# Value products of an attention kernel kept whole, in other banks, with the orders of a pair of units rewritten

## The chip, the cores and the metric

The kernel runs on one core of a Trainium2 chip. The core has five engines with an instruction stream of their own each: TensorE (PE, matrix products into PSUM), VectorE (DVE), ScalarE (ACT), GpSimd (POOL) and SyncE (SP, which issues DMAs). They wait for each other through semaphores alone, and within an engine instructions run in the order in which they are written. The metric is the time of one execution on the device in microseconds (us); lower is better.

## What is computed

```python
def _L0_xattn_ref(query, kv, Wq, bq, Wkv, bkv, Wo, bo):      # query: layernorm(x), 32 x 64 x 512; kv: ctx
    q = (query @ Wq + bq).reshape(B, L, NKV, G, HDIM)         # 8 key heads, 4 query heads each, HDIM 128
    k_, v_ = jnp.split(kv @ Wkv + bkv, 2, axis=-1)
    ...
    scores = jnp.einsum('blkgd,bmkd->bkglm', q, k) * scale
    attn = jax.nn.softmax(scores, axis=-1)
    o = jnp.einsum('bkglm,bmkd->blkgd', attn, v).reshape(B, L, NHEAD * HDIM)
    return o @ Wo + bo
...
x = x + _L0_xattn_ref(_layernorm(x), ctx, ...)
x = x + _L0_ffn_ref(_layernorm(x), router_w, router_b, A, Bm)   # 8 low-rank experts, best 2 of each token
```

## The kernel before

All is in float32. Each product that needs full accuracy is made of passes of rounded parts: a factor is split into a high part (made on ACT, `high`, L819) and a low part (the rest: source minus high part, made on DVE, L1155, or on POOL, L592), and PE multiplies high by high, low by high and high by low (L1675 to L1677).

The work goes over 8 groups (one key head and its 4 query heads) of 4 units of 512 tokens (8 batch rows of 64). Two units are a **duo**, d; its units are 2d and 2d+1. A group has two duos, p=0 and p=1; the loop runs groups 1 to 6, both duos of group 7 stand written out behind it, and `opening()` does the first two duos. Each engine has its own function `duo(g, p)`, in which the order is written by hand; nothing is scheduled by a planner. In duo d four things overlap:

- **Query products** of duo d: seven products of a Strassen-like scheme (`product(k, r)`, k = 1, 6, 2, 7, 4, 5, 3, in two halves r) instead of eight. ACT copies the first (`first_product`), DVE adds the others up (`y_sum`, `z_sum`, `w_sum`, `query_sum`) to the four blocks c11, c21 (unit 2d) and c12, c22 (unit 2d+1); ACT makes their high part (`query_high`), POOL the low part (`query_low`).
- **Scores** of units 2d and 2d+1, each in two halves c (`scores(d, k, c)`), into the four banks `att`.
- **Softmax** of each half (u, c): ACT copies half of the scores (`copy_half`), DVE adds the other half (`s_add`), transposes and takes the row maximum (`s_max`), ACT swaps partitions (`swap_max`, four short copies), DVE takes the peak (`s_peak`), POOL subtracts (`shift`), ACT exponentiates (`exponents`), DVE sums (`s_sum`), ACT swaps (`swap_sum`), DVE inverts (`s_inverse`, two short instructions), POOL multiplies (`normalise`), DVE transposes back (`p_turn`), ACT and POOL split the result (`probs_high`, `probs_low`). Halves c of successive units use the same memory, so `copy_half(u+1, c)` comes behind `p_turn(u, c)`.
- **Value products** of units 2d-2 and 2d-1 (`outputs(u, c)`, twelve matmuls of 256 columns) into the two banks `turn`, split on ACT (`output_high`) and DVE (`output_low`), and the eight **output tiles** of these units (`out(d, p, j)`, j = 0 to 3 and 4 to 7), which DVE adds to `y` (`add`).

PSUM's other banks are a `ring` of four, which query products and output tiles share. In the second duo of a group ACT and POOL also split Wo, and, but in the last group, DVE combines the next group's query weights (`combine_w`, L1208 to L1216, in `parts` from `raw`) and ACT and POOL split these (`split_q`). The last group's second duo also begins the statistics of the second layernorm. SP's queue loads blocks of x (`load_block`), keys, values and weights in a fixed order, each behind a semaphore.

On PE, value products stood alone between query products or output tiles: c=0 of unit 2d-2 behind product (6,1), c=1 behind (4,0), c=0 of unit 2d-1 behind `scores(d, 0, 1)`, c=1 behind `out(d, p, 3)`.

## Time and profile before

| | |
|---|---|
| time, median of 3 runs | 1061.63 us (1060.66 to 1062.37) |
| profiled execution, its own time | 1060.89 us |
| span of its records | 1058.7 us |
| PE, DVE, POOL, ACT busy | 98%, 76%, 64%, 53% of the span |
| granted TensorE clock, mean | 0.995 of full |

Busy shares are means over the whole span. Ends of matmuls are modelled and overlap, so the spacing of PE's work is read from starts. A row of a timeline may merge several equal instructions (x2, x4); `<-` before a name says which engine and line ended an idle time.

### The profile page before, as it was taken

The numbers are of one execution on the slowest core, as the hardware profiler recorded it, in microseconds if no ns is written. First come the engines' busy times: TensorE is split into PE (matmuls) and PEld (weight loads), VectorE is DVE, ScalarE is ACT, GpSimd is POOL, SyncE is SP. The second block draws the span as 40 slices with busy tenths as digits, with TensorE's granted clock in tenths as the row PEclk, the third lists the DMA queues.
The fourth block names the chain that finished last, engine by engine and source line by source line (L and its number), as shares of the span: only waits on it lengthen the run. The fifth ranks groups of instructions, "written<-read, shape, count | busy, mean of one in ns | idle before, by whom it ended". The sixth has DMA issues, their size and how long they took to land.

```text
span 1058.7 us, 17316 instructions
## 1 busy us (share of the span) xinstructions
PE 1035.8 (98%) x5409; PEld 850.4 (80%) x5409; DVE 802.0 (76%) x1420; ACT 557.2 (53%) x1314; POOL 674.5 (64%) x563
## 2 busy tenths in 40 slices
PE   8999999988999999999999999999999999999996
PEld 7878887867788888888888888888888888887884
DVE  3563455469987887797788878877987797788986
ACT  3122113257756665665567566666665575665420
POOL 1286237768876787677578767866786787574300
PEclk9999999999999999999999999999999999999998
DMA  8647963995364655546282827364554637240013
GB/s 310 208 129 256 317 212 82 394 352 200 130 255 149 220 179 187 204 152 258 99 290 89 314 96 261 133 234 143 213 218 148 241 115 270 94 154 11 2 41 120
DMA packets 85657, 197.99 MB, mean 187 GB/s; under 512 B 10560, under 2 KB 43368, under 8 KB 70384
## 3 DMA queue, kind: packets, MB, share of 16 engines
q1 hardware_dynamic: 83072, 181.73, 49.4%
q10 hardware_dynamic: 2544, 15.73, 3.7%
q8 instruction: 23, 0.38, 0.1%
q14 instruction: 18, 0.15, 0.0%
HBM read 161.78 MB, written 35.65 MB: 186 GB/s over the span
## 4 chain that ended last, share of the span: by engine, by line
PE 79%; DVE 9%; DMA 6%; POOL 3%; issue 1%; ACT 1%; SPq 1%; ACTq 0%; DVEq 0%
PE banks L1675 23%; PE banks L1676 22%; PE banks L1677 22%; PE banks L1815 5%; PE banks L1798 2%; PE banks L1799 2%; DMA k_raw<-keys_dram 2%; PE banks L1700 1%; DMA values_dram<-parts 1%; DMA keys_dram<-parts 1%; DVE stats L1230 1%; DMA raw<-in_L_xattn_Wq_dram 1%; DVE xo L1155 1%; POOL w_l L592 1%; DMA raw<-in_L_xattn_Wkv_dram 1%
## 5 line engine op out<-in xcount | busy, mean ns | idle before, releaser
L1675 PE MATMUL banks<-wo_h,xo 128*128 128x512 f32 x512 | 204.5, 399 | 0.0
L1676 PE MATMUL banks<-wo_l,xo 128*128 128x512 f32 x512 | 200.5, 392 | 0.0
L1677 PE MATMUL banks<-wo_h,xo 128*128 128x512 f32 x512 | 199.9, 390 | 0.0
L592 POOL TENSOR_TENSOR qT_l<-parts,qT_h 128x512 fp32r<-128x512 f32 x128 | 165.4, 1298 | 52.1 <-ACT qT_h L819 52.1
L1675 PE MATMUL banks<-xo,w_h 128*128 128x512 f32 x448 | 179.0, 400 | 2.5 <-DVE parts L1280 1.9
L1676 PE MATMUL banks<-xo,w_h 128*128 128x512 f32 x448 | 175.7, 392 | 0.0
L1677 PE MATMUL banks<-xo,w_l 128*128 128x512 f32 x448 | 174.4, 389 | 0.0
L592 POOL TENSOR_TENSOR xo<-sT,xo 128x512 fp32r<-128x512 f32 (+1 forms) x72 | 102.6, 1425 | 75.5 <-ACT xo L819 75.5
L1155 DVE TENSOR_TENSOR xo<-banks,xo 128x512 fp32r<-128x512 f32 (+1 forms) x156 | 100.8, 665 | 31.2 <-ACT xo L819 30.7
L1675 PEld LDWEIGHTS banks<-wo_h,xo 128*128 128x128 f32 x512 | 96.5, 188 | 23.5 <-issue 0.2
L1303 DVE SCALAR_TENSOR_TENSOR parts<-banks,g_bias,parts 128x512 f32<-128x512 f32 x128 | 94.6, 741 | 26.8 <-PE banks L1677 24.4
L1677 PEld LDWEIGHTS banks<-wo_h,xo 128*128 128x128 f32 x512 | 96.4, 188 | 21.0
L1676 PEld LDWEIGHTS banks<-wo_l,xo 128*128 128x128 f32 x512 | 96.6, 189 | 18.3
L819 ACT ACTIVATE xo<-banks 128x512 fp32r<-128x512 f32 (+1 forms) x156 | 84.8, 581 | 39.8 <-PE banks L1815 21.8
L819 ACT ACTIVATE qT_h<-parts 128x512 fp32r<-128x512 f32 x128 | 80.2, 629 | 47.8 <-DVE parts L1303 46.1
L1350 DVE TENSOR_TENSOR y<-banks,y 128x512 f32<-128x512 f32 x120 | 81.2, 682 | 31.4 <-PE banks L1677 30.8
L625 POOL TENSOR_TENSOR low_or_x<-low_or_x,row_sum 128x512 f32<-128x512 f32 x64 | 70.5, 1102 | 53.7 <-DVE row_sum L1339 53.7
L1675 PEld LDWEIGHTS banks<-xo,w_h 128*128 128x128 f32 x448 | 84.2, 188 | 24.0 <-DVE parts L1280 2.3
L618 POOL TENSOR_TENSOR low_or_x<-low_or_x,row_max 128x512 f32<-128x512 f32 x64 | 70.2, 1097 | 47.1 <-DVE row_max L1325 46.0
L1677 PEld LDWEIGHTS banks<-xo,w_l 128*128 128x128 f32 x448 | 84.1, 188 | 18.6
L1676 PEld LDWEIGHTS banks<-xo,w_h 128*128 128x128 f32 x448 | 84.2, 188 | 15.2
L917 ACT COPY low_or_x<-banks 64x512 f32<-64x512 f32 x64 | 37.3, 583 | 109.3 <-PE banks L1799 109.2
(145 smaller groups left out, 2269.4 us busy)
## 6 DMA issues: line engine op xcount, KB each, us to landing
xo<-x_dram SPq DMA_DIRECT2D x105, 1024.0 KB, 5.0
x_dram<-xo ACTq DMA_DIRECT2D x14, 1024.0 KB, 11.9
values_dram<-parts SPq DMA_DIRECT2D x64, 128.0 KB, 2.9
keys_dram<-parts SPq DMA_DIRECT2D x32, 256.0 KB, 5.0
k_raw<-keys_dram SPq DMA_DIRECT2D x32, 256.0 KB, 4.9
raw<-in_L_xattn_Wo_dram SPq DMA_DIRECT2D x8, 1024.0 KB, 8.0
v_raw<-values_dram SPq DMA_DIRECT2D x64, 128.0 KB, 3.7
raw<-in_L_xattn_Wkv_dram SPq DMA_DIRECT2D x7, 1024.0 KB, 6.7
```

Source lines behind the costliest of these rows:

```text
L592: return nc.gpsimd.tensor_tensor(dst, src, high_part.bitcast(F32), ALU.subtract)
L618: nc.gpsimd.tensor_tensor(s[:, blocks, :], s[:, blocks, :], row_max[:, blocks].unsqueeze(2).broadcast_to([P, D // QR, QR]), ALU.subtract). ...
L625: nc.gpsimd.tensor_tensor(s[:, blocks, :], s[:, blocks, :], row_sum[:, blocks].unsqueeze(2).broadcast_to([P, D // QR, QR]), ALU.mult).then ...
L819: return nc.scalar.activation(dst, src, ACT.Copy)
L917: act.copy(half[L:P, c], att_s[L:P, :, 0, :])
L1155: return nc.vector.tensor_tensor(dst, src, high_part.bitcast(F32), ALU.subtract)
L1303: nc.vector.scalar_tensor_tensor(out=slot_of(c, r), in0=product_of(d, p, k, r), scalar=q_bias(c, r), in1=slot_of(what, r), op0=ALU.add, op ...
L1350: nc.vector.tensor_tensor(y[:, t, :], ring[:, slot, :], y[:, t, :], ALU.add).then_inc(y_added, 1)
L1675: mm(dst, stat[0], mov[0], start=start, stop=False)
L1676: mm(dst, stat[0], mov[1], start=False, stop=False)
L1677: return mm(dst, stat[1], mov[0], start=False, stop=stop)
L1815: last = mm(turn[:, i, n % 2 * G * L:(n % 2 + 1) * G * L], v[keys_of, n, :], p[keys_of, n, :], start=p is pT_h and v is v_h, stop=p is pT_l)
```

## The change

Value products are made whole: both halves c of a unit follow each other on PE. Unit 2d-2 has its place behind product (7,1); unit 2d-1 behind `out(d, p, 3)`, and behind it follow product (3,1) and `scores(d, 0, 1)`, which stood earlier. One half of each unit goes to other banks (`value_bank`): c=0 of unit 2d-2 into the score banks, c=1 of unit 2d-1 into ring slots 2 and 3. Ring slots become fixed per duo (`OUT_SLOTS`), with other semaphores waited for. The orders on ACT, DVE and POOL are rewritten to this, `query_high` of c12 r=1 comes last (`HIGHS`), weight combinations and their splits move, and combination 2 lies in another part of memory (slot 2 of `parts` instead of 0). In the tail's order DVE has the first output lows ahead of a row maximum. The opening and the work of each instruction are as before.

```diff
+OUT_SLOTS = (2, 3, 1, 0, 0, 1, 2, 3)
+PV_SLOTS = (2, 3)
...
+            return isinstance(d, int) and d < DUOS
+
+        def product_slot(d, p, k, r):
+
+            return ((DUO_TASKS * p if opening_duo(d) else 0) + PROD_AT[k, r]) % RING
+
+        def out_slot(d, p, j):
+
+            return (DUO_TASKS * p + len(PROD) + j) % RING if opening_duo(d) else OUT_SLOTS[j]
+
+        def value_bank(d, k, c, i):
+
+            if d is not None and k == 0 and c == 0:
+                return att[:, i, :]
+            if d is not None and k == 1 and c == 1:
+                return ring[:, PV_SLOTS[i], :]
+            return turn[:, i, :]
...
+                if split:
+                    split_q(g + 1, [0, 2], False)
+                normalise(2 * d, 0)
                 query_low(d, "c12", 1)
                 keys_low(2 * d + 1)
+                if split:
+                    split_q(g + 1, [1], False)
                 shift(2 * d, 1)
-                normalise(2 * d, 0)
...
-                    split_q(g + 1, [0], False)
+                    split_q(g + 1, [3], False)
                 values_low(2 * d)
...
-                output_high(2 * d - 2, 0, 0)
-                output_high(2 * d - 2, 0, 1)
                 query_high(d, "c11", 0)
                 swap_sum(2 * d - 1, 0)
                 wo_high_part(3)
                 query_high(d, "c11", 1)
                 exponents(2 * d - 1, 1)
                 swap_sum(2 * d - 1, 1)
-                output_high(2 * d - 2, 1, 0)
+                output_high(2 * d - 2, 0, 0, d, 0)
+                output_high(2 * d - 2, 0, 1, d, 0)
+                output_high(2 * d - 2, 1, 0, d, 0)
+                output_high(2 * d - 2, 1, 1, d, 0)
                 query_high(d, "c21", 0)
-                output_high(2 * d - 2, 1, 1)
...
+                query_high(d, "c12", 0)
+                query_high(d, "c22", 1)
+                probs_high(2 * d - 1, 1)
                 copy_half(2 * d, 0)
                 if split:
                     split_q(g + 1, [0], False)
-                probs_high(2 * d - 1, 1)
-                query_high(d, "c12", 0)
-                query_high(d, "c12", 1)
-                copy_half(2 * d, 1)
                 swap_max(2 * d, 0)
-                query_high(d, "c22", 1)
-                output_high(2 * d - 1, 0, 0)
-                output_high(2 * d - 1, 0, 1)
-                swap_max(2 * d, 1)
                 exponents(2 * d, 0)
-                keys_high(2 * d + 1)
-                output_high(2 * d - 1, 1, 0)
-                output_high(2 * d - 1, 1, 1)
-                swap_sum(2 * d, 0)
-                exponents(2 * d, 1)
                 if split:
                     split_q(g + 1, [2], False)
+                swap_sum(2 * d, 0)
+                output_high(2 * d - 1, 0, 0, d, 1)
+                output_high(2 * d - 1, 0, 1, d, 1)
+                output_high(2 * d - 1, 1, 0, d, 1)
+                output_high(2 * d - 1, 1, 1, d, 1)
+                copy_half(2 * d, 1)
+                query_high(d, "c12", 1)
+                keys_high(2 * d + 1)
+                if split:
+                    split_q(g + 1, [1, 3, 5], False)
+                swap_max(2 * d, 1)
+                probs_high(2 * d, 0)
+                exponents(2 * d, 1)
+                copy_half(2 * d + 1, 0)
+                swap_sum(2 * d, 1)
                 values_high(2 * d)
-                swap_sum(2 * d, 1)
-                probs_high(2 * d, 0)
-                copy_half(2 * d + 1, 0)
                 if split:
-                    split_q(g + 1, [1, 3, 5, 4, 6], False)
+                    split_q(g + 1, [4, 6], False)
                 probs_high(2 * d, 1)
                 if not last:
+                    swap_max(2 * d + 1, 0)
                     copy_half(2 * d + 1, 1)
-                if not last:
-                    swap_max(2 * d + 1, 0)
...
-                        dve.wait_ge(q_low, 16 * g)
+                        dve.wait_ge(q_low, 16 * g - 8 + LOW_AT["c21", 0])
                     ins = nc.vector.tensor_tensor(s1, w_block(1, 0), w_block(1, 1), ALU.add)
...
                     ins = nc.vector.tensor_tensor(s3, w_block(0, 0), w_block(1, 0), ALU.subtract)
                 else:
                     dve.wait_ge(combined, 4 * g + 2)
...
@@ -1262,7 +1285,7 @@
...
                 s_peak(2 * d - 1, 1)
                 query_sum(d, p, "c11", 0)
                 query_sum(d, p, "c11", 1)
-                output_low(2 * d - 2, 0, 0)
-                output_low(2 * d - 2, 0, 1)
                 s_inverse(2 * d - 1, 0)
                 z_sum(g, d, p, 0)
                 z_sum(g, d, p, 1)
                 s_sum(2 * d - 1, 1)
                 query_sum(d, p, "c21", 0)
+                output_low(2 * d - 2, 0, 0, d, 0)
+                output_low(2 * d - 2, 0, 1, d, 0)
                 query_sum(d, p, "c21", 1)
                 p_turn(2 * d - 1, 0)
                 w_sum(d, p, 0)
                 query_sum(d, p, "c22", 0)
                 w_sum(d, p, 1)
-                output_low(2 * d - 2, 1, 0)
+                output_low(2 * d - 2, 1, 0, d, 0)
                 query_sum(d, p, "c22", 1)
                 s_inverse(2 * d - 1, 1)
-                add(0)
-                output_low(2 * d - 2, 1, 1)
+                output_low(2 * d - 2, 1, 1, d, 0)
                 p_turn(2 * d - 1, 1)
                 query_sum(d, p, "c12", 0)
+                if split:
+                    combine_w(g + 1, 1, False)
+                add(0)
                 s_add(2 * d, 0)
-                query_sum(d, p, "c12", 1)
                 s_max(2 * d, 0)
                 add(1)
-                s_add(2 * d, 1)
                 s_peak(2 * d, 0)
-                s_max(2 * d, 1)
-                output_low(2 * d - 1, 0, 0)
-                output_low(2 * d - 1, 0, 1)
+                if split:
+                    combine_w(g + 1, 2, False)
                 add(2)
-                s_peak(2 * d, 1)
                 s_sum(2 * d, 0)
                 if split:
-                    combine_w(g + 1, 1, False)
-                output_low(2 * d - 1, 1, 0)
+                    combine_w(g + 1, 3, False)
                 add(3)
-                if split:
-                    combine_w(g + 1, 2, False)
+                output_low(2 * d - 1, 0, 0, d, 1)
+                output_low(2 * d - 1, 0, 1, d, 1)
                 s_inverse(2 * d, 0)
-                output_low(2 * d - 1, 1, 1)
-                s_sum(2 * d, 1)
+                output_low(2 * d - 1, 1, 0, d, 1)
+                query_sum(d, p, "c12", 1)
+                output_low(2 * d - 1, 1, 1, d, 1)
+                s_add(2 * d, 1)
+                s_max(2 * d, 1)
                 p_turn(2 * d, 0)
-                if split:
-                    combine_w(g + 1, 3, False)
                 add(4)
-                add(5)
-                if last:
-                    ln_stats("f", 0)
-                s_inverse(2 * d, 1)
+                s_peak(2 * d, 1)
                 if split:
                     combine_w(g + 1, 4, False)
+                if last:
+                    add(5)
+                    for t in range(3):
+                        tile_stats("f", t)
+                s_sum(2 * d, 1)
                 s_add(2 * d + 1, 0)
+                s_inverse(2 * d, 1)
+                if last:
+                    tile_stats("f", 3)
+                    ln_combine("f", 0)
+                if not last:
+                    add(5)
+                    s_max(2 * d + 1, 0)
+                if not last:
+                    add(6)
                 p_turn(2 * d, 1)
                 if not last:
-                    add(6)
-                    s_max(2 * d + 1, 0)
                     add(7)
-                if not last:
                     s_add(2 * d + 1, 1)
 
 
...
+                elif (k, r) == (3, 1) and not opening_duo(d):
+                    pe.wait_ge(y_added, d * 8 - 8 + 3)
...
+                if k == 0 and c == 0 and not opening_duo(d):
+                    pe.wait_ge(o_low, (2 * d - 2) * 4 + 2)
...
-            def outputs(u, c):
+            def outputs(u, c, d=None, k=None):
 
                 pe.wait_ge(v_low, u + 1)
                 pe.wait_ge(p_low, u * 2 + c + 1)
-                if not isinstance(u, int) or u > 0 or c > 0:
+                if d is not None and k == 0 and c == 0:
+                    pe.wait_ge(s_added, u * 2 + 4)
+                elif d is not None and k == 1 and c == 1:
+                    pe.wait_ge(y_added, d * 8 - 8 + 2)
...
-                            last = mm(turn[:, i, n % 2 * G * L:(n % 2 + 1) * G * L], v[keys_of, n, :], p[keys_of, n, :],
+                            last = mm(value_bank(d, k, c, i)[:, n % 2 * G * L:(n % 2 + 1) * G * L], v[keys_of, n, :], p[keys_of, n, :],
                                       start=p is pT_h and v is v_h, stop=p is pT_l)
                             if n % 2 and p is pT_l:
                                 last.then_inc(o_filled, 1)
 
             def out(d, p, j):
 
-                if j < 4:
+                if opening_duo(d) and j < 4:
                     pe.wait_ge(summed, d * len(SUMS) + SUM_AT[("c22", "c12")[j // 2], j % 2])
+                elif opening_duo(d):
+                    pe.wait_ge(y_added, d * 8 - 8 + j - 4 + 1)
+                elif j in (0, 1, 2, 3, 5):
+                    name, r = {0: ("c22", 0), 1: ("c22", 1), 2: ("c21", 1), 3: ("c12", 0), 5: ("c12", 1)}[j]
+                    pe.wait_ge(summed, d * len(SUMS) + SUM_AT[name, r])
+                elif j == 4:
+                    pe.wait_ge(y_added, d * 8 - 8 + 4)
                 else:
-                    pe.wait_ge(y_added, d * 8 - 8 + j - 4 + 1)
-                out_project(2 * d - 2 + j // UT, out_slot(p, j), j % UT)
+                    pe.wait_ge(o_low, (2 * d - 1) * 4 + 3 + j - 6)
+                out_project(2 * d - 2 + j // UT, out_slot(d, p, j), j % UT)
 
             def opening():
...
                 product(g, p, 6, 0)
                 product(g, p, 6, 1)
-                outputs(2 * d - 2, 0)
                 product(g, p, 2, 0)
                 product(g, p, 2, 1)
                 product(g, p, 7, 0)
                 product(g, p, 7, 1)
+                outputs(2 * d - 2, 0, d, 0)
+                outputs(2 * d - 2, 1, d, 0)
                 product(g, p, 4, 0)
-                outputs(2 * d - 2, 1)
                 product(g, p, 4, 1)
                 product(g, p, 5, 0)
                 product(g, p, 5, 1)
@@ -1899,13 +1945,13 @@
                     pe.wait_ge(wo_low, (STEPS + g) * KC + KC)
                 out(d, p, 0)
                 scores(d, 0, 0)
-                product(g, p, 3, 1)
                 out(d, p, 1)
-                scores(d, 0, 1)
-                outputs(2 * d - 1, 0)
                 out(d, p, 2)
                 out(d, p, 3)
-                outputs(2 * d - 1, 1)
+                outputs(2 * d - 1, 0, d, 1)
+                outputs(2 * d - 1, 1, d, 1)
+                product(g, p, 3, 1)
+                scores(d, 0, 1)
                 out(d, p, 4)
                 out(d, p, 5)
                 scores(d, 1, 0)
```

Three places show how instructions move. First PE in the first duo of a group, around the value products of unit 2d-2. Before (L1677 is a query product, L1815 the value product; ISA and REGISTER_ALU are the sequencer's):

```order
L1677 MATMUL banks<-xo,w_l 128x512
L1805 ISA
L1806 ISA
L1808 REGISTER_ALU
L1815 MATMUL banks<-xo,v_h 128x256 x2
L1815 MATMUL banks<-xo,v_l 128x256 x2
L1815 MATMUL banks<-xo,v_h 128x256 x4
L1815 MATMUL banks<-xo,v_l 128x256 x2
L1815 MATMUL banks<-xo,v_h 128x256 x2
L1761 REGISTER_ALU
L1764 REGISTER_ALU
```

In the changed kernel (its line numbers are larger by some tens: L1706 query product, L1854 value product):

```order
L1854 MATMUL banks<-xo,v_h 128x256 x2
L1854 MATMUL banks<-xo,v_l 128x256 x2
L1854 MATMUL banks<-xo,v_h 128x256 x4
L1854 MATMUL banks<-xo,v_l 128x256 x2
L1854 MATMUL banks<-xo,v_h 128x256 x2
L1839 REGISTER_ALU
L1845 REGISTER_ALU
L1854 MATMUL banks<-xo,v_h 128x256 x2
L1854 MATMUL banks<-xo,v_l 128x256 x2
L1854 MATMUL banks<-xo,v_h 128x256 x4
L1854 MATMUL banks<-xo,v_l 128x256 x2
L1854 MATMUL banks<-xo,v_h 128x256 x2
```

A second value product follows at once; before, another query product came first.

Then ACT in the same duo, around `copy_half(2d, 0)` (COPY low_or_x, two rows). `qT_h<-parts` are high parts of c blocks, `xo<-sT` those of probabilities. Before, from c22 r=0 on:

```order
L819 ACTIVATE qT_h<-parts 128x8x64
L819 ACTIVATE xo<-sT 128x512
L916 ISA
L917 COPY low_or_x<-banks 64x512
L918 COPY low_or_x<-banks 64x512
L819 ACTIVATE xo<-sT 128x512
L881 REGISTER_ALU
L819 ACTIVATE qT_h<-parts 128x8x64
L881 REGISTER_ALU
L819 ACTIVATE qT_h<-parts 128x8x64
```

In the changed kernel:

```order
L837 ACTIVATE qT_h<-parts 128x8x64
L837 ACTIVATE xo<-sT 128x512
L899 REGISTER_ALU
L837 ACTIVATE qT_h<-parts 128x8x64
L899 REGISTER_ALU
L837 ACTIVATE qT_h<-parts 128x8x64
L837 ACTIVATE xo<-sT 128x512
L934 ISA
L935 COPY low_or_x<-banks 64x512
L936 COPY low_or_x<-banks 64x512
```

The copy moved behind both halves' probabilities of unit 2d-1 and behind two more high parts.

Last DVE in the second duo of a group, behind the peak of (2d, 0) (row_max<-row_max,other). `parts<-...raw` are weight combinations, row_sum the row sum, y an output tile's add. Before, further down, combination 1 stands behind a row sum:

```order
L1325 TENSOR_TENSOR row_max<-row_max,other 128x16
L1331 TENSOR_REDUCE row_sum<-low_or_x 128x16
L1202 ISA
L1207 REGISTER_ALU
L1208 TENSOR_TENSOR parts<-raw 128x512
L1354 REGISTER_ALU
L1155 TENSOR_TENSOR xo<-banks,xo 128x2x4x64
L1350 TENSOR_TENSOR y<-banks,y 128x512
L1210 ISA
```

In the changed kernel combination 2 stands behind the peak:

```order
L1348 TENSOR_TENSOR row_max<-row_max,other 128x16
L1229 ISA
L1231 REGISTER_ALU
L1232 TENSOR_TENSOR parts<-parts,raw 128x512
L1373 TENSOR_TENSOR y<-banks,y 128x512
L1354 TENSOR_REDUCE row_sum<-low_or_x 128x16
L1234 TENSOR_TENSOR parts<-raw 128x512
L1373 TENSOR_TENSOR y<-banks,y 128x512
```

Combination 2 moved up to the peak, and combination 3 to the place behind the row sum.

## Rows read from the trace of the kernel before

**Rows 1.** The page's shares: busy us, share of the span, instructions of each engine
```profile
PE 1035.8 (98%) x5409; PEld 850.4 (80%) x5409; DVE 802.0 (76%) x1420; ACT 557.2 (53%) x1314; POOL 674.5 (64%) x563
```

**Rows 2.** Windows of two successive duos: busy us of PE, PEld, DVE, ACT, POOL; clock, DMA
```profile
477.57:526.90 49.33, 49.33 (x263) 40.51 (x261) 39.31 (x69) 28.22 (x70) 34.26 (x29) 1.00 0.52 191
526.90:576.22 49.32, 49.32 (x262) 40.50 (x261) 41.92 (x69) 33.79 (x81) 38.17 (x31) 1.00 0.53 191
```

**Rows 3.** Timeline of PE around a value product: start, us, engine, line, operation
```profile
531.91 0.39 PE L1676 MATMUL banks<-xo,w_h 128*128 128x512 f32 x1
...
532.14 0.39 PE L1677 MATMUL banks<-xo,w_l 128*128 128x512 f32 x1
...
532.46 0.38 PE L1815 MATMUL banks<-xo,v_h 64*128 64x256 f32 x2
...
532.68 0.28 PE L1815 MATMUL banks<-xo,v_l 64*128 64x256 f32 x2
...
533.36 0.50 PE L1675 MATMUL banks<-xo,w_h 128*128 128x512 f32 x1
...
533.70 0.40 PE L1676 MATMUL banks<-xo,w_h 128*128 128x512 f32 x1
```

**Rows 4.** Instructions by line and shape over both duos: busy, mean ns, idle before
```profile
L1303 DVE SCALAR_TENSOR_TENSOR parts<-banks,g_bias,parts 128x512 f32<-128x512 f32 x16 | 11.9, 742 | 3.9 <-PE banks L1677 3.8
...
L819 ACT ACTIVATE qT_h<-parts 128x512 fp32r<-128x512 f32 x16 | 10.1, 630 | 5.6 <-DVE parts L1303 5.3
...
L1320 DVE TENSOR_REDUCE row_max<-low_or_x 128x16 f32<-128x512 f32 x9 | 6.2, 686 | 0.3
...
L1344 DVE STREAM_TRANSPOSE sT<-low_or_x 128x512 f32<-128x512 f32 x8 | 5.7, 707 | 0.1
...
L1313 DVE TENSOR_TENSOR sT<-banks,low_or_x 64x512 f32<-64x512 f32 x8 | 5.6, 695 | 0.1
...
L1155 DVE TENSOR_TENSOR xo<-banks,xo 128x512 fp32r<-128x512 f32 x16 | 10.5, 677 | 1.2 <-ACT xo L819 1.1
...
L927 ACT ACTIVATE low_or_x<-low_or_x 128x512 f32<-128x512 f32 x8 | 5.0, 630 | 0.8 <-POOL low_or_x L618 0.5
...
L917 ACT COPY low_or_x<-banks 64x512 f32<-64x512 f32 x8 | 4.7, 583 | 15.3 <-PE banks L1799 15.3
...
L910 ACT COPY other<-row_max 32x16 f32<-32x16 f32 x16 | 3.2, 202 | 3.4 <-DVE row_max L1320 3.2
...
L1339 DVE RECIPROCAL row_sum<-row_sum 128x16 f32<-128x16 f32 x8 | 2.0, 253 | 0.3
...
L1465 DVE COPY g_bias<-bias 128x4 f32 x1 | 0.2, 170 | 0.0
```

**Rows 5.** Timeline of DVE in two places
```profile
484.43 0.68 DVE L1331 TENSOR_REDUCE row_sum<-low_or_x 128x16 f32<-128x512 f32 x1
...
485.02 0.83 DVE L1325 TENSOR_TENSOR row_max<-row_max,other 128x16 f32<-128x16 f32 x1
...
562.77 1.28 DVE L1208 TENSOR_TENSOR parts<-raw 128x512 f32<-128x512 f32 x1
```

**Rows 6.** Timeline of ACT: two activations in a row
```profile
502.56 0.63 ACT L819 ACTIVATE xo<-sT 128x512 fp32r<-128x512 f32 x1
503.11 0.63 ACT L819 ACTIVATE qT_h<-parts 128x512 fp32r<-128x512 f32 x1
```

**Rows 7.** Timeline of POOL in the places of rows 5
```profile
483.26 2.56 POOL L592 TENSOR_TENSOR w_l<-parts,w_h 128x512 fp32r<-128x512 f32 x2
...
559.91 1.05 POOL L618 TENSOR_TENSOR low_or_x<-low_or_x,row_max 128x512 f32<-128x512 f32 x1
...
563.46 1.50 POOL L618 TENSOR_TENSOR low_or_x<-low_or_x,row_max 128x512 f32<-128x512 f32 x1
```

**Rows 8.** DMA issues: tensor, queue, count, KB each, median us to landing
```profile
xo<-x_dram SPq DMA_DIRECT2D x105, 1024.0 KB, 5.0
...
raw<-in_L_xattn_Wq_dram SPq DMA_DIRECT2D x7, 1024.0 KB, 5.6
```

More of the change, by code:

```diff
@@ L63 @@
 SUM_AT = {name: n + 1 for n, name in enumerate(SUMS)}
-HIGHS = [("c11", 0), ("c11", 1), ("c21", 0), ("c21", 1), ("c22", 0), ("c12", 0), ("c12", 1), ("c22", 1)]
+HIGHS = [("c11", 0), ("c11", 1), ("c21", 0), ("c21", 1), ("c22", 0), ("c12", 0), ("c22", 1), ("c12", 1)]
 HIGH_AT = {name: n + 1 for n, name in enumerate(HIGHS)}
@@ L765, in duo @@
                 if split:
[L766 removed]
+                    split_q(g + 1, [6], False)
             split_wo(0, range(KC))
@@ L876, in first_product @@
                     act.wait_ge(q_low, d * 8 - 4)
-                act.copy(slot_of("x", r), ring[:, product_slot(p, 1, r), :]).then_inc(copied, 1)
+                act.copy(slot_of("x", r), ring[:, product_slot(d, p, 1, r), :]).then_inc(copied, 1)
             def query_high(d, c, r):
@@ L1210, in combine_w @@
                     dve.wait_ge(combined, 4 * g + 1)
+                    if not first:
+                        dve.wait_ge(q_low, 16 * g - 8 + LOW_AT["c12", 0])
                     ins = nc.vector.tensor_tensor(s2, s1, w_block(0, 0), ALU.subtract)
@@ L1215, in combine_w @@
                     dve.wait_ge(combined, 4 * g + 2)
+                    if not first:
+                        dve.wait_ge(q_low, 16 * g - 8 + LOW_AT["c22", 1])
                     ins = nc.vector.tensor_tensor(s4, w_block(0, 1), s2, ALU.subtract)
```

49 lines of the change are left out of this document (24 added, 25 removed), and 2 rows, old and new, of the table VECTOR_TAIL.

## The prediction

> **What bounds the kernel now.** I read the page's shares first: TensorE (PE) is busy for 98% of the span [rows 1]. Then the windows of two successive duos in the middle of the main loop: PE is busy for 49.33 of 49.33 us and for 49.32 of 49.32, the granted clock is full, while VectorE (DVE) has 39.3 and 41.9, GpSimd (POOL) 34.3 and 38.2, ScalarE (ACT) 28.2 and 33.8 [rows 2]. So in the loop nothing is waited for on PE, and its 14 duos are 14 x 49.33 = 690.6 us of the 1058.7 us span. An edit there can win in two ways only: less PE time, or nothing. It can lose wherever another engine now comes later than PE.
>
> **What PE saves.** The reader is to look at starts, since ends of matmuls are modelled. A 512-column matmul follows the last by 0.23 us; the one ahead of a value product is followed after 0.32; the twelve value matmuls take 0.90, of which the first two 0.22; and the first matmul behind them is followed after 0.34 [rows 3]. Leaving and entering thus costs 0.09 + 0.11, some 0.06 more in the next ten matmuls, and inside the block 0.1 at the first and 0.1 at the last pair, since the four steady pairs between take about 0.115 each: 0.46 per block. Two of four blocks in a duo now follow directly on another, and the switch from scores to a value product goes: 2 x 0.46 = 0.9 less, 48.45 us a duo. If PE stays the bound that is 14 x 0.88 = 12.3 us.
>
> **What the other engines then need.** The new order ties the three elementwise engines into one chain that goes round once per duo and touches PE nowhere decisively. I follow it from the start of the DVE sum for c12, half r=0 (time 0). Durations are those of [rows 4]; followers on one engine start closer than they last: DVE 0.60 apart [rows 5], ACT 0.54 [rows 6]. A handover between engines I take as 0.03 (the stall of a peak that I come to ends 0.03 after its cause [rows 5, 7]), to POOL 0.08.
>
> First stretch, the half (2d,0). The sum lasts 0.74. ACT then has three activations in a row before `copy_half(2d,0)`, which stood ahead of all three: 0.74 + 0.03 + 3 x 0.54 = 2.39. Copy 0.60 + 0.58 (to 3.57), s_add 0.70 + 0.73 (5.02), transpose and row maximum 0.74 + 0.69 (6.45), swap of four copies 0.85 (7.33), peak, which ends at 7.65 (below), shift 1.05 (8.78), exponent 0.63 (9.44), row sum 0.68 (10.15), swap 0.87: the first `output_high` of unit 2d-1 starts at 11.06. Before, two of the four stood ahead of that exponent and two ahead of that swap; now all four stand behind both. Its DVE half starts at 11.69, the second at 12.29 and ends at 12.97. `out(d,4)` waits for it. On PE that tile is 12.4 us behind the first scores (three output tiles, two value blocks, one query product, one score half); so at once it is late by several tenths, even if everything else were early.
>
> Second stretch. DVE: low, low, inverse (0.21 + 0.17), low, c12 r=1, low take 3.45; s_add of half (2d,1) starts at 15.14. Add and row maximum 2.87, p_turn and one add 1.3, peak 19.32, shift, exponent at 20.66, and only behind that exponent ACT copies the scores of (2d+1,0): s_add 22.4. Then inverse 0.46, an add, row maximum, an add, p_turn at 26.84 (1.42 + 0.46 + 0.6 + 1.34 + 0.6), probs_high 0.63, swap 0.87, and only then `copy_half(2d+1,1)`: its s_add starts at 30.31. PE passed the end of the duo at about 26.0 (out4 at 13.15 + 12.84 us of the rest), so this half is some 4 us behind its scores.
>
> Third stretch, in the next duo. s_add 1.42, peak, y 0.7, row maximum 1.34, y 0.6, row sum 0.6: peak at 34.97, held by POOL to 35.6; c11 0.74, its activation 0.66, swap 0.88, inverse at 37.86; two z sums and the row sum 2.4, swap 0.87: `output_high` at 41.16, low at 41.79. Then nine DVE instructions to the inverse, 5.8, normalise 1.05, p_turn, and the next c12 sum at 49.8.
>
> So one turn takes 49.8 us where PE needs 48.45 and needed 49.33. PE's own events lie clear of it: c21 r=0 needs product (4,0), which arrives at 40.35, and has until 41.1.
>
> **The port between DVE and POOL.** A DVE peak of 16 elements lasted 0.83 us, from 485.02 to 485.85, and POOL's running pair of low parts ended at 485.82 [rows 5, 7]. In the other direction, a DVE combination of two SBUF operands ran from 562.77 to 564.05, and the POOL shift begun at 563.46 took 1.50 instead of 1.05 [rows 5, 7]. So peaks and inverses (two SBUF inputs) wait for POOL's running instruction, and weight combinations hold back POOL. Both bear on the chain now. Peak (2d,0) finds the last of four low parts running; the peak of (2d-1,1) finds a Wo or key part. In the six duos that also split the next group's weights, combinations 2 and 4 stand directly behind a peak whose shift the chain waits for: 0.35 and 0.32 each, and combination 3 (up to 0.4) ahead of the add and low behind it. The duo after such a one has the group's bias copy (0.17 [rows 4] and its own wait, 0.3 together) and an inverse that meets a low part (0.45). 49.8 becomes 51.1 there, 0.5 of it with even chances either way.
> The Trainium skill (SBUF — State Buffer, "Who interferes with whom") says that a DVE instruction with two SBUF inputs and a GpSimd instruction that reads SBUF exclude each other for the whole instruction, whichever began first. The trace agrees in kind. By that rule each shift would be held for all of a combination (0.68), which adds 0.35 x 2 x 6 = 4 us to the sum; I keep the 0.45 that the row shows as the most.
>
> **The sum.** From the loop's first product to the first c12 sum 23.1 us (there PE still leads: product (4,0) at 14.3, then 8.7 of DVE); 7 turns of 49.8 and 6 of 51.1, 655.2; from the last c12 sum to PE's end of the loop 26.0: 704.3. That is 13.6 more than 690.6. The tail's first low part and p_turn come about 0.5 later in relation to PE. The profiled execution took 1060.9 us (0.7 under the median of 1061.6), so 1075.0 for its like, and I say 1075.
>
> **Edits costed at nothing.** Value products in score and ring banks wait for s_add of (2d-1,1), for add 1 and for older low parts; by the walk these end 5, 1.5 and 10 us before PE asks; product (3,1) needs add 2 and has only some tenths, which fall into PE's wait ahead of the fifth tile in any case. POOL's new places for split parts lie where it waits for an inverse. The blocks for products 2 and 7 of the next duo are issued behind product (3,1), which moves from 25 to 34.6 us in its duo; they land within 5.0 us [rows 8] and are needed at 53.9. Combination 1 now stands at 0.7, and the next group's raw weights are issued 6.9 before time 0 and land in 5.6 [rows 8]: at worst it starts some tenths later and still ends before s_add at 3.6. The SP queue holds no other issue behind these that anyone needs sooner. If this cover fails, the whole wait adds, since combination, add and s_add are in one queue.
>
> **Rivals.** (1) The chain is shorter than I walked and PE stays the bound: faster. For: DVE is busy for only 41.9 of 49.3 us in the fuller duo [rows 2], and 70 steps with 0.02 us of error each one way would make 1.4 us. Against: the durations repeat to a few ns. At best 1061.6 - 12.3 = 1049.3; but even with the first and third stretch free, low parts held back to 12.97 bind PE through product (4,0), c21 and the c12 sum in 48.9 a duo, which gives 1055.6. (2) The chain turns in about 49.3: 1061 to 1063, no change to be told. (3) The port's coin flips all fall badly: the inverse at 37.86 just misses POOL's gap and waits for the next low part (1.25 us, 7 times), combination 3 waits for a split part (0.8, 6 times): 13.6 us more at most, half of it likely in that case: 1083. It decides where two instructions are ready within 0.05 us of each other. (4) The change removes no switch, as PE cannot run two value blocks back to back because the second waits for its bank: then even (1) is void and the time is that of the chain, 1075.
>
> **How the numbers follow.** My forecast 0.55 (1066 to 1081 by itself); (3) 0.19; (2) 0.10; (1) 0.16. (4) changes none of these, since the chain sets the time. What can be told from no change is about 0.2%, 2.1 us. Faster 0.16, same 0.10, slower 0.74. The range leaves out about 0.13 below and 0.07 above: 1056 to 1088.
>
> **What the profile will show.** Right: in the loop PE waits once or twice per duo, above all ahead of the fifth output tile for the DVE low part and slightly ahead of the first; ACT hardly waits for scores any more (its copies waited 15.3 us for them in two duos [rows 4]); a duo takes 49.8 to 51.5. Joined value blocks take about 1.6 us for 24 matmuls. Wrong: a loop of 48.5 to 49.2 us per duo with PE fully busy; or PE waiting for a DMA, or at half clock, which I expect nowhere new in the loop.

## The result and the profile after

The changed kernel takes 1094.15 us (median of 4 runs, 1091.17 to 1094.61) against 1061.14 for the kernel before in the same session: 1.0319 times as long, 95% interval 1.0301 to 1.0337. The forecast was 1075.0 with a range to 1088: right in its sign and in what it said would wait, too small by 19 us and outside its range.

The page's shares, to be held against [rows 1]:

```profile
PE 1038.0 (95%) x5409; PEld 853.2 (78%) x5409; DVE 798.1 (73%) x1420; ACT 557.2 (51%) x1314; POOL 671.1 (62%) x563
```

No engine has more instructions, and only PE and its weight loads are busy for longer (by 2.2 and 2.8 us); all have a smaller share of a span of 1088.9 us. Windows cut at the start of the c12 r=0 sum, the point from which the prediction walked its chain ("a turn"): first the turn from a group's first duo into its second, then the one that starts in the second and splits weights (columns as in [rows 2]):

```profile
716.08:767.19 51.11, 49.38 (x262) 40.43 (x261) 38.70 (x67) 30.26 (x74) 33.53 (x29) 1.00 0.47 170
767.19:819.42 52.23, 50.14 (x262) 41.57 (x261) 41.60 (x73) 31.73 (x77) 38.34 (x32) 0.97 0.56 195
```

The turns alternate between 51.1 and 52.2, where before a duo took 49.33 and the walk had said 49.8 and 51.1. PE now waits; its two dearest waits over the whole run (us in total, how often, the longest):

```profile
PE banks L1704 <- DVE xo L1174: 20.5, 16, 2.1
...
PE banks L1704 <- DVE parts L1326: 8.6, 10, 0.9
```

The first is mostly the fifth output tile waiting for its low part, the second the first output tile. The copies of scores on ACT, which waited 15.3 us in two duos [rows 4], wait no more (last columns: idle time ahead and its cause):

```profile
L935 ACT COPY low_or_x<-banks 64x512 f32<-64x512 f32 x8 | 4.6, 581 | 0.2
```

The place that decides. The first inverse of a group's second duo on DVE, and POOL at the same time:

```profile
754.13 1.28 DVE L1359 TENSOR_TENSOR row_sum<-row_sum,other 128x16 f32<-128x16 f32 x1 [0.90 <-ACT other L929]
```

```profile
753.08 1.06 POOL L632 TENSOR_TENSOR low_or_x<-low_or_x,row_max 128x512 f32<-128x512 f32 x1
754.09 1.30 POOL L606 TENSOR_TENSOR qT_l<-parts,qT_h 128x512 fp32r<-128x512 f32 x1
```

POOL began the c11 low part at 754.09; the inverse was released at 754.13, 0.04 later, and lasted until POOL was done (755.39): 1.28 us for 16 elements a row. It is so in all seven turns that end in a second duo: 0.04 or 0.05 behind POOL, 1.28 or 1.29 long.

In the split turn, combinations 2 (L1232) and 3 (L1234) on DVE, and POOL beside them:

```profile
774.69 0.18 DVE L1348 TENSOR_TENSOR row_max<-row_max,other 128x16 f32<-128x16 f32 x1 [0.19 <-ACT other L929]
774.89 0.69 DVE L1232 TENSOR_TENSOR parts<-parts,raw 128x512 f32<-128x512 f32 x1
...
777.79 1.80 DVE L1234 TENSOR_TENSOR parts<-raw 128x512 f32<-128x512 f32 x1
```

```profile
774.95 1.54 POOL L632 TENSOR_TENSOR low_or_x<-low_or_x,row_max 128x512 f32<-128x512 f32 x1 [0.21 <-DVE row_max L1348]
776.45 1.30 POOL L606 TENSOR_TENSOR w_l<-raw,w_h 128x512 fp32r<-128x512 f32 x1
777.75 1.29 POOL L606 TENSOR_TENSOR w_l<-parts,w_h 128x512 fp32r<-128x512 f32 x1
...
787.94 1.43 POOL L632 TENSOR_TENSOR low_or_x<-low_or_x,row_max 128x512 f32<-128x512 f32 x1 [0.44 <-DVE row_max L1348]
```

Combination 2 holds the shift back by 0.49 (1.54 for 1.05), and combination 3 again comes 0.04 after POOL has begun: 1.80 instead of 0.69. Combination 4, behind the next peak, holds the shift of (2d,1) by 0.38 (the last line, 1.43 for 1.05).

On PE, the joined value product (to be held against [rows 3]):

```profile
753.41 0.38 PE L1854 MATMUL banks<-xo,v_h 64*128 64x256 f32 x2
...
755.02 0.50 PE L1704 MATMUL banks<-xo,w_h 128*128 128x512 f32 x1
```

From 753.41 to 755.02 it is 1.61 us for 24 matmuls; twice 0.90 before.

### The profile page after: what moved, and what is told of

The parts are those of the page before. It is cut to its first block, busy times and chain, and to the rows that moved or that the text cites. A ratio compares the mean times of both kernels' runs of the same rounds, so it can differ in the third digit from the quotient of the medians.

```text
span 1088.9 us, 17332 instructions
## 1 busy us (share of the span) xinstructions
PE 1038.0 (95%) x5409; PEld 853.2 (78%) x5409; DVE 798.1 (73%) x1420; ACT 557.2 (51%) x1314; POOL 671.1 (62%) x563
## 4 chain that ended last, share of the span: by engine, by line
DVE 39%; PE 16%; issue 14%; POOL 12%; ACT 10%; DMA 6%; DVEq 1%; SPq 1%; ACTq 0%; POOLq 0%
PE banks L1704 5%; DVE parts L1326 5%; PE banks L1706 5%; PE banks L1705 5%; DVE xo L1174 4%; POOL low_or_x L632 3%; DVE sT L1336 3%; DVE low_or_x L1341 3%; DVE y L1373 3%; DVE sT L1367 2%; DVE sT L1335 2%; POOL qT_l L606 2%; DVE row_sum L1359 2%; DVE row_sum L1354 2%; ACT xo L837 2%
## 5 line engine op out<-in xcount | busy, mean ns | idle before, releaser
L1706 PE MATMUL banks<-wo_h,xo 128*128 128x512 f32 x512 | 201.5, 394 | 0.0
L1706 PE MATMUL banks<-xo,w_l 128*128 128x512 f32 x448 | 174.4, 389 | 0.0
L1704 PEld LDWEIGHTS banks<-wo_h,xo 128*128 128x128 f32 x512 | 97.7, 191 | 56.0 <-DVE xo L1174 20.1
L1706 PEld LDWEIGHTS banks<-wo_h,xo 128*128 128x128 f32 x512 | 97.5, 190 | 21.3
L639 POOL TENSOR_TENSOR low_or_x<-low_or_x,row_sum 128x512 f32<-128x512 f32 x64 | 67.7, 1058 | 71.0 <-DVE row_sum L1362 71.0
L632 POOL TENSOR_TENSOR low_or_x<-low_or_x,row_max 128x512 f32<-128x512 f32 x64 | 72.7, 1136 | 54.8 <-DVE row_max L1348 53.6
L1706 PEld LDWEIGHTS banks<-xo,w_l 128*128 128x128 f32 x448 | 84.1, 188 | 18.2
L1705 PEld LDWEIGHTS banks<-xo,w_h 128*128 128x128 f32 x448 | 84.2, 188 | 15.3
L1335 DVE TENSOR_TENSOR sT<-banks,low_or_x 64x512 f32<-64x512 f32 x64 | 43.7, 683 | 70.5 <-ACT low_or_x L936 69.8
L837 ACT ACTIVATE xo<-sT 128x512 fp32r<-128x512 f32 (+1 forms) x72 | 48.5, 674 | 90.0 <-DVE sT L1367 56.0
L837 ACT ACTIVATE xo<-banks 128x512 fp32r<-128x512 f32 (+1 forms) x156 | 80.8, 590 | 21.3 <-PE banks L1729 8.6
```

The source lines that it names most:

```text
L632: nc.gpsimd.tensor_tensor(s[:, blocks, :], s[:, blocks, :], row_max[:, blocks].unsqueeze(2).broadcast_to([P, D // QR, QR]), ALU.subtract). ...
L639: nc.gpsimd.tensor_tensor(s[:, blocks, :], s[:, blocks, :], row_sum[:, blocks].unsqueeze(2).broadcast_to([P, D // QR, QR]), ALU.mult).then ...
L837: return nc.scalar.activation(dst, src, ACT.Copy)
L1335: nc.vector.tensor_tensor(whole[0:L], att_s[0:L, :, 0, :], half[L:P, c], ALU.add)
L1704: mm(dst, stat[0], mov[0], start=start, stop=False)
L1705: mm(dst, stat[0], mov[1], start=False, stop=False)
```

## The experiments

Each kernel ran five times (E5 and E8 twelve times); there is no E7. Ratios are to the kernel before in the same session, which took 1058.9 us for E1 to E4, 1059.3 for E5, E6 and E8, 1059.9 for E9 and E10 and 1060.5 for E11 and E12; so kernels are compared by ratios and by the turns of their traces, not by their times alone. Turns are given as unsplit, split; the last of each kind can differ by 0.3. Theory A: the chain through ACT, DVE and POOL sets the loop, and its excess over the walk is port waits. Theory B: TensorE's own round trip sets it.

| kernel | time, us | ratio to before (95%) | turns, us |
|---|---|---|---|
| changed | 1094.15 | 1.0319 (1.0301 to 1.0337) | 51.1, 52.2 |
| E1 inverse clear | 1085.38 | 1.0245 (1.0231 to 1.0259) | 50.6, 51.9 |
| E2 combination 3 moved | 1092.03 | 1.0305 (1.0291 to 1.0319) | 51.2, 52.1 |
| E3 copy first | 1079.89 | 1.0188 (1.0172 to 1.0203) | 49.4, 52.1 to 52.8 |
| E4 changed, one pair parted | 1094.43 | 1.0329 (1.0315 to 1.0343) | 51.2, 52.2 |
| E6 weight work moved | 1093.36 | 1.0318 (1.0298 to 1.0338) | 51.1, 52.5 |
| E5 = E1 + E3 + E6 | 1062.91 | 1.0025 (1.0012 to 1.0038) | 48.8, 50.3 |
| E8 = E5, one pair parted | 1062.60 | 1.0027 (1.0016 to 1.0037) | 48.8, 50.4 |
| E9 chain short | 1049.33 | 0.9907 (0.9892 to 0.9921) | 48.4, 48.4 |
| E10 = E9, one pair parted | 1052.78 | 0.9937 (0.9923 to 0.9950) | 48.8, 48.8 |
| E11 weight work again | 1085.25 | 1.0233 (1.0219 to 1.0247) | 51.2, 51.1 |
| E12 = E9, copy late again | 1066.74 | 1.0059 (1.0045 to 1.0074) | 49.8, 49.7 |

**E1.** POOL's order, both duos of a group:

```diff
+                normalise(2 * d - 1, 0)
                 query_low(d, "c11", 0)
                 if p == 1:
                     split_wo(STEPS + g, [2])
-                normalise(2 * d - 1, 0)
```

> GpSimd takes the product for half (2d-1,0) (normalise) ahead of the low part of c11 r=0, so that the inverse in front of it finds GpSimd idle. Theory A (the chain through ScalarE, VectorE and GpSimd sets the loop, and what it has over the walk is two port waits that fell badly): the inverse that lasted 1.28 us in the turns of 51.13 takes about 0.2 and those turns fall to about 50.1; in the other turns it took 0.50 and they fall by 0.3 (52.2 to 51.9). 7 x 1.05 + 6 x 0.3 = 9 us less than the changed kernel's 1094: about 1085. Theory B (TensorE's own round trip over product 4, the c21 and c12 sums and the fifth output tile sets the loop, and the inverse has slack): no change, 1092 to 1096.

The time is theory A's number, but only in part by the expected way, and in part by the faster session: the 13 turns fell by 5.7 us together, not by 9. The inverse finds POOL idle; the next one, of (2d-1,1), does not:

```profile
750.98 0.18 DVE L1359 TENSOR_TENSOR row_sum<-row_sum,other 128x16 f32<-128x16 f32 x1 [0.91 <-ACT other L929]
...
760.48 0.91 DVE L1359 TENSOR_TENSOR row_sum<-row_sum,other 128x16 f32<-128x16 f32 x1
```

It lasted 0.42 in the changed kernel; about half of the 1.10 gained is given back there, and the turn falls by 0.55.

**E2.** DVE's order:

```diff
-                if split:
-                    combine_w(g + 1, 3, False)
                 add(3)
                 output_low(2 * d - 1, 0, 0, d, 1)
                 output_low(2 * d - 1, 0, 1, d, 1)
+                if split:
+                    combine_w(g + 1, 3, False)
```

> The third weight combination moves behind the first two output lows, where GpSimd waits for the inverse and the port is free. Theory A: its 1.80 us become 0.68, the fifth output tile's low part comes 1.7 us earlier in the six split duos, the inverse 1.1 earlier, and the turns of 52.2 fall to 51.1; 6 x 1.1 = 6.6 less: about 1087.5. Theory B: the fifth tile waits less, but the turn stays at 52.2: 1092 to 1096.

This is what theory B said, and not theory A: the turn lost 0.1, not 1.1. The trace has a reason that leaves theory A standing, and E4 and E12 below speak against theory B. The combination took 0.68, but the low part behind it began only 0.70 earlier, since ACT's high part, late through the held shift, came last; and in its new place the combination stands ahead of the inverse.

**E3.** ACT's order, and POOL's:

```diff
+                copy_half(2 * d, 0)
                 query_high(d, "c12", 0)
                 query_high(d, "c22", 1)
                 probs_high(2 * d - 1, 1)
-                copy_half(2 * d, 0)
...
                 query_low(d, "c22", 0)
+                shift(2 * d, 0)
                 query_low(d, "c12", 0)
                 query_low(d, "c22", 1)
-                shift(2 * d, 0)
```

> ScalarE copies the scores of (2d,0) ahead of the three high parts that stand in front of it, and GpSimd takes the shift of that half ahead of two query low parts. Theory A: the first stretch of the chain is 2.2 us shorter (first output low at about 9.5 instead of 11.7 after the c12 sum), TensorE no longer waits ahead of the fifth tile, and the half (2d,1) then follows its scores (13.3 instead of 15.2): turns of about 49.3 and 50.3, 13 turns some 25 us less: about 1069. Theory B (TensorE's round trip is the bound at 51): the lateness moves to the query low parts and the time falls by less than 8 us, 1086 to 1094.

The time lies between the two theories' numbers. The turn without weights falls to 49.4 as expected. The split one does not: combination 2 waits for the c12 low part, since it overwrites its source, and that part now comes behind the shift:

```profile
769.50 1.76 DVE L1232 TENSOR_TENSOR parts<-parts,raw 128x512 f32<-128x512 f32 x1 [2.41 <-POOL qT_l L606]
```

It waited 2.41 us for it, and then for the port (1.76 for 0.69), with the row sum of the half queued behind: the gain was turned into a new wait. That the split turns differ here, 52.1 or 52.8, comes from combination 3. It is ready 0.02 behind POOL's start, and in two of the six split duos it waits, in the other four POOL does. DVE and POOL in one duo of each kind:

```profile
365.83 1.82 DVE L1234 TENSOR_TENSOR parts<-raw 128x512 f32<-128x512 f32 x1
...
467.99 0.68 DVE L1234 TENSOR_TENSOR parts<-raw 128x512 f32<-128x512 f32 x1
```

```profile
365.82 1.29 POOL L606 TENSOR_TENSOR w_l<-parts,w_h 128x512 fp32r<-128x512 f32 x1
...
467.97 1.85 POOL L606 TENSOR_TENSOR w_l<-parts,w_h 128x512 fp32r<-128x512 f32 x1
```

**E4.** On PE, in the changed kernel:

```diff
-                product(g, p, 7, 1)
                 outputs(2 * d - 2, 0, d, 0)
+                product(g, p, 7, 1)
                 outputs(2 * d - 2, 1, d, 0)
```

> The two halves of unit 2d-2 are parted on TensorE again by half a product (7,1): one switch of 0.46 us more in every duo. Theory A (TensorE waits for the chain in every duo, 0.8 us or more ahead of the first output tile): nothing changes, 1092 to 1096, and the wait shrinks by about 0.4. If TensorE set the loop: 14 x 0.46 = 6.4 us more, 1100.

As theory A said: the turns are the same to 0.1 us, the ratio is 0.1% higher, within its interval, where 6.4 us would be 0.6%. The wait ahead of the first output tile shrinks from 8.6 us in all to 4.8. In the changed kernel the switch saved on PE is worth nothing.

**E6.** In DVE's order combination 1 goes behind add(2), 2 behind add(3), 3 behind the peak of (2d,1), 4 behind add(7); the bias copy behind the row sum of (2d-1,0); the split parts on ACT follow; on POOL, of the first parts:

```diff
-                    split_q(g + 1, [0, 2], False)
+                    split_q(g + 1, [0], False)
                 normalise(2 * d, 0)
+                if split:
+                    split_q(g + 1, [2], False)
                 query_low(d, "c12", 1)
                 keys_low(2 * d + 1)
+                shift(2 * d, 1)
                 if split:
                     split_q(g + 1, [1], False)
-                shift(2 * d, 1)
                 probs_low(2 * d, 0)
```

> The changed kernel with the next group's weight work alone moved: the four combinations to places where VectorE idles and GpSimd holds no shift (1 behind the third output add, 2 behind the fourth, 3 behind the peak of (2d,1) and its add, 4 behind the eighth add), their splits behind them, and the bias copy behind the row sum of (2d-1,0). Theory A (what the split duos have over the others is combinations and their port waits standing in the chain: shift held 0.5, combination 3 in the queue 0.6, shift held again 0.4, bias copy 0.3): turns of 52.2 fall to about 50.6, those of 51.13 stay: 6 x 1.6 = 9.6 less, about 1083 beside 1093. Theory B (the split turns are longer for another reason, such as ScalarE's seven extra high parts or the weight transfer): less than 3 us, 1090 to 1094.

No gain: the time is theory B's, though E11 will show that its reason does not hold. The first stretch did get shorter: s_add of (2d,1) starts 15.21 behind the c12 sum, where it was 16.39 in the changed kernel. Two new waits took it back: the next s_add waits for probabilities' low parts, ahead of which the edit had put a split part, and the bias copy pushed the peak onto POOL's next instruction. Combination 3, now directly behind the peak of (2d,1), also holds its shift as combination 4 did (1.43). The two new waits:

```profile
792.12 0.68 DVE L1340 TENSOR_TENSOR sT<-banks,low_or_x 64x512 f32<-64x512 f32 x1 [1.15 <-POOL xo L606]
...
804.82 0.48 DVE L1498 COPY g_bias<-bias 128x4 f32 x1
...
805.34 1.22 DVE L1353 TENSOR_TENSOR row_max<-row_max,other 128x16 f32<-128x16 f32 x1
```

**E5 and E8.** The three edits together, and the same with E4's.

> All of it together: the copy of (2d,0) first and its shift early, the product for (2d-1,0) ahead of the c11 low part, the weight work moved. Theory A: the chain falls under TensorE's own 48.45, or near it: turns of 48.5 to 49.3, TensorE nearly without waits, 7 x 2.3 + 6 x 3.0 = 34 less than 1093, about 1059, as the kernel before within 4 us. Theory B (TensorE's round trip over the c21 and c12 sums and the fifth tile holds the loop at 49.5 or more): 1066 to 1072.

> As e5_all, with the value product of unit 2d-2 parted again on TensorE by half a product. If TensorE sets the loop of e5_all, the switch costs what the prediction's account of switches says, 0.46 us in each duo: 14 x 0.46 = 6.4 us more than e5_all. If a chain of the other engines still sets that loop, it costs less, 0 to 3 us.

The three together give back almost all: 0.25% over the kernel before, as theory A said. The turn without weights comes down to 48.8; the other keeps E6's new waits. Parting the pair costs nothing in the one and 0.15 in the other: the chain still sets this loop.

**E9 and E10.** E5 with five more edits: the bias copy for the next group at the end of the second duo, combination 3 behind the row sum of (2d,1), in a first duo the keys' low part behind that of c11 r=0, and on POOL the split parts from 1 on and the values' low part later:

```diff
                 probs_low(2 * d, 0)
                 if split:
                     normalise(2 * d, 1)
+                    split_q(g + 1, [1], False)
                     values_low(2 * d)
...
-                values_low(2 * d - 1)
                 query_low(d, "c21", 1)
                 normalise(2 * d - 1, 1)
+                values_low(2 * d - 1)
```

> e5_all with what its split turns (50.27 where the others take 48.79) still had in the chain moved out: the bias copy into the idle time at the end of the group's second duo, combination 3 behind the row sum of (2d,1) so that no shift is held, the split part 1 behind the product for (2d,1) instead of ahead of the low part of the probabilities (which released the next s_add 0.8 late), keys' low part behind the first shift, values' low part behind the product for (2d-1,1) whose inverse lasted 0.93. Theory A: all turns fall to TensorE's own 48.45 to 48.8; against e5_all 6 x 1.6 + 7 x 0.2 = 11 less: about 1052, faster than the kernel before by 0.6 to 0.8%. Theory B (TensorE's round trip holds at 49 or more): 1056 to 1060.

> As e9_chain_short, with the value product of unit 2d-2 parted again on TensorE. If TensorE now sets the loop, one switch costs 0.46 us a duo as in the prediction's account: turns of 48.9, 14 x 0.46 = 6.4 us more than e9_chain_short. If e9's turns are still those of the chain (48.8), about 2 us more.

Two turns of E9, then of E10:

```profile
689.07:737.48 48.41, 48.41 (x262) 40.44 (x262) 37.58 (x68) 30.18 (x74) 33.61 (x29) 1.00 0.54 199
737.48:785.87 48.39, 48.39 (x262) 40.41 (x261) 42.17 (x73) 31.64 (x77) 38.55 (x32) 1.00 0.55 191
```

```profile
692.78:741.61 48.83, 48.83 (x262) 40.39 (x262) 37.74 (x67) 30.19 (x74) 33.59 (x29) 1.00 0.53 197
741.61:790.44 48.83, 48.83 (x262) 40.40 (x262) 42.03 (x72) 31.65 (x77) 38.54 (x32) 1.00 0.53 191
```

In both PE is busy throughout. E9 is faster than the kernel before, by 0.9% (0.8 to 1.1), and a switch costs 0.43 us a duo on PE (48.83 less 48.40). The medians are 3.5 us apart where 14 such duos make 6.0; the two runs whose traces are shown are 6.5 apart, and single runs of E9 spread over 3.1.

**E11 and E12.** E11 makes E9's edits on the weight work alone (and puts the keys' low part behind the first product); E12 is E9 with E3's edit undone. Against E11, E12 has only POOL's order changed, in two places: the product for (2d-1,0) ahead of the c11 low part, and that for (2d-1,1) ahead of the values' low part.

> The weight work of the changed kernel moved as in e9_chain_short, and nothing else of it: the copy of (2d,0) stays behind the three high parts, the inverse of (2d-1,0) still meets the c11 low part. Theory A (the split turns have 1.1 us more because combinations, their port waits and the bias copy stand in the chain): they fall to the others' 51.1, or a little over: 6 x 1.1 = 6.6 less, about 1086. Theory B (they are longer for another reason): 1091 to 1095.

> e9_chain_short with the copy of (2d,0) put back behind the three high parts and its shift behind four low parts. Theory A: the first stretch is 1.9 us longer again (s_add of (2d,1) at 15.2 instead of 13.4 behind the c12 sum), the port waits stay away: the chain takes about 50.0 a turn, the walk's 49.8 with its handovers 0.2 longer; TensorE waits ahead of the fifth output tile; 14 x 1.6 = 22 more than e9_chain_short, about 1071. Theory B (after the port waits are gone the chain has slack): within 5 us of e9_chain_short.

E11: both kinds of turn take 51.1, so what the split ones had more was the weight work. The inverse that took 0.50 in one kind now takes 1.29 in both. Its first and second inverse in one duo:

```profile
750.17 1.29 DVE L1365 TENSOR_TENSOR row_sum<-row_sum,other 128x16 f32<-128x16 f32 x1 [0.91 <-ACT other L933]
...
760.74 0.44 DVE L1365 TENSOR_TENSOR row_sum<-row_sum,other 128x16 f32<-128x16 f32 x1
```

E12, two turns, and the same two inverses:

```profile
700.16:749.97 49.81, 49.13 (x262) 40.33 (x262) 37.50 (x67) 30.27 (x74) 33.57 (x29) 1.00 0.54 191
749.97:799.72 49.75, 49.03 (x262) 40.27 (x261) 41.44 (x73) 31.74 (x77) 38.05 (x32) 1.00 0.54 185
```

```profile
738.24 0.18 DVE L1365 TENSOR_TENSOR row_sum<-row_sum,other 128x16 f32<-128x16 f32 x1 [0.91 <-ACT other L933]
...
747.73 0.16 DVE L1365 TENSOR_TENSOR row_sum<-row_sum,other 128x16 f32<-128x16 f32 x1
```

With the changed kernel's order of copies and highs and both inverses clear of POOL, a turn takes the 49.8 us of the walk, with PE waiting 0.7 in it. The pair E11 and E12 shows the cause: 1.3 us a turn come and go with the two waits. The time is 4 under the 1071 expected of E12, as its turns are 0.2 shorter than the 50.0 said.

## Why the prediction was wrong

**Right: what bounds, and where PE waits.** The chain through ACT, DVE and POOL sets the loop (E4: a PE switch more costs nothing; E12: with the inverses clear it takes 49.8). The walk's points hold to 0.2 us up to the first inverse: s_add of (2d,1) at 15.21 for 15.14, the s_add two halves later at 30.52 for 30.31, the inverse at 38.06 for 37.86. PE waits ahead of the fifth tile and of the first, and in the loop nowhere else for more than 0.5 us, so the edits costed at nothing cost PE nothing that shows.

**Right: what PE saves.** 0.46 a switch and 48.45 a duo were said; E10 less E9 gives 0.43, and E9's duo is 48.40. Rival (1) gave 1049.3 for a loop bound by PE. E9, whose loop PE does bind after a new order on ACT, DVE and POOL, takes 0.9907 of the kernel before, which is 1051.7 on the prediction's 1061.6; that its own median is 1049.33 is luck, since its session was 1.7 us faster. The rival's limit of 48.9 a duo rests on low parts that end 12.97 behind the c12 sum; in E9 the copy comes first and the inverse behind two of them starts at 11.2 to 11.6 where it started at 12.9 to 14.1.

**Wrong: the size of the port term.** The step that failed is "49.8 becomes 51.1 there, 0.5 of it with even chances either way": it put 1.3 us into the split turns and, beyond the held peaks that the walk has in every turn, nothing into the others. The inverse at 37.86 was left to rival (3). What this rival names happened in every duo that it names, and it was too small as well: its 13.6 us at most give 1088.6 (half of them give 1081.8, not the 1083 said). It has combination 3 at 0.8 where it waited 1.11, and lacks the second inverse. Where the time went is read from starts: PE's first product of the loop in the kernel before and in the changed one, and the first and the last c12 sum of the changed one on DVE:

```profile
280.27 0.39 PE L1675 MATMUL banks<-xo,w_h 128*128 128x512 f32 x1
```

```profile
278.12 0.40 PE L1704 MATMUL banks<-xo,w_h 128*128 128x512 f32 x1
```

```profile
302.69 0.71 DVE L1326 SCALAR_TENSOR_TENSOR parts<-banks,g_bias,parts 128x512 f32<-128x512 f32 x1
...
973.32 0.71 DVE L1326 SCALAR_TENSOR_TENSOR parts<-banks,g_bias,parts 128x512 f32<-128x512 f32 x1
```

The loop begins 2.1 earlier than before (278.1 for 280.3); from there to the first c12 sum it is 24.6 us for the 23.1 said (+1.5); the 13 turns take 670.6 for 655.2 (+15.4); the rest to the end of the span is 115.6 for 114.3 (26.0, before's 87.8 of tail, and 0.5; +1.3). Together +16.1, and the profiled run took 1091.2 for the 1075.0 said. The median lies 3.0 above that run. A run of 1094.4 has them ahead of the loop: in E4, whose turns are the same, the loop begins at 280.87 instead of 278.12.

The +1.5 is the port term too: the two inverses in that stretch took 1.29 and 0.42, and in E12, where they take 0.18 and 0.17, it is 23.2 us (278.7 to 301.9).

The 15.4 are two terms. Seven turns took 1.3 more than the walk's 49.8 (the last of them 1.0): the first inverse 1.28 instead of 0.18, the second 0.42 instead of 0.16. With both waits gone E12 stands at 49.8. Six turns took 1.1 more than the 51.1 said for them (one of them 0.8). What they have over 49.8 was mis-sized at 1.3 and is 2.4: the first inverse 0.50 instead of 0.18 and the second as above, 0.6 together; combinations 2 and 3, 1.18 (16.39 less 15.21 in E6); the shift held by combination 4, 0.38 (1.43 for 1.05); the bias copy ahead of a peak, 0.3. E11 takes the weight work out of the chain, and both kinds of turn then meet the same inverse of 1.29: the split one falls by 1.1 although this inverse grew by 0.8, so the weight work had cost 1.9, which is what its three terms make.

Why a mean was wrong: the order is fixed and the durations repeat to some hundredths. POOL runs from the shift behind the peak of (2d-1,0) to the c11 low part without a pause, and the inverse hangs on the same peak, 6.1 us behind it in all seven turns; so it lost by 0.04 or 0.05 each time. It is one toss for seven or six places, as long as the lead repeats. With a lead of 0.02 for POOL it did not: combination 3 in E3 fell both ways, two to four. The prediction had named a release within 0.05 us of POOL's next instruction as the point that decides; its walk had the inverse at 37.86, 0.2 us too early, and POOL's low part began at 38.01.

The Trainium skill (SBUF — State Buffer, "Who interferes with whom") calls the port pair an exclusive lock in which the loser is blocked for the whole of the other's instruction. The trace agrees for DVE: 1.28 us for an inverse that alone takes 0.18. For POOL the block was 0.14 shorter than that: until the end of combination 2 (775.58) the shift would have been held for 0.63, and it lost 0.49. The two held shifts, 0.35 and 0.32 in the prediction, came to 0.49 and 0.38.

**Open.** How E1 and E3 lost part of their saving further on is read from their traces and not tested apart, and which of E9's five edits matters how much on top of E5 is not known. The +1.3 behind the last c12 sum is not taken apart; it is 115.0 us in E12 and 114.0 in E9.

## What to carry to other kernels

Where several in-order engines form a chain that is longer than the matmuls, taking work off TensorE buys nothing; first make the chain shorter than TensorE's own time per turn, here by putting the instruction that starts a half ahead of those with slack, and work for later where the waiting engine idles. Price a race between instructions of fixed length as all or nothing over the whole loop, unless the lead is as small as the spread of the durations. And check each instruction moved for what it overwrites and who is behind it: three of these edits lost some or all of their gain in a later wait.

## What was not expected of the hardware

In three of the six split duos the granted clock fell behind PE's longest wait. PE around the fifth output tile:

```profile
779.07 0.28 PE L1832 MATMUL banks<-qT_l,kT 128*128 128x256 f32 x1
781.44 0.79 PE L1704 MATMUL banks<-wo_h,xo 128*128 128x512 f32 x1 [2.09 <-DVE xo L1174]
782.03 0.63 PE L1705 MATMUL banks<-wo_l,xo 128*128 128x512 f32 x1
782.46 0.63 PE L1706 MATMUL banks<-wo_h,xo 128*128 128x512 f32 x1
...
784.93 0.40 PE L1706 MATMUL banks<-wo_h,xo 128*128 128x512 f32 x1
```

After 2.09 us of idling the granted clock was 0.51 from 781.4 to 784.9, the level of 1.2 GHz: matmuls follow each other at 0.43 (0.23 otherwise), and the tiles take about 1.5 us longer. In the other three a wait as long (2.08 to 2.10) left the clock alone. E4's trace has the fall in the same three duos. The turns with the fall are no longer than those without (52.2), since PE had that time to spare. The prediction had expected half clock nowhere new in the loop.
